# Attention outputs of a unit go raw through a DRAM scratch, are packed by DMA and normalised in packed form

## The chip, the cores and the metric

One core of a Trainium2 chip runs the whole program in one launch. The metric is the device time of one execution in microseconds. The kernel before took 4148.24 us (median of three runs, 4138.67 to 4152.86).

## What is computed

The input is a batch of 8 sequences of 1024 tokens, width 256. Four attention levels with 16 heads of width 16 read every token, every second, every fourth and every eighth; the results are merged from the coarse level to the fine one (linear upsampling, a projection, an addition), the input is added, and a layernorm follows. Then comes a feed-forward net with a gated layer, two hidden layers of 1024 and a second layernorm.

```python
for lvl in range(4):
    x = query[:, ::2 ** lvl, :]
    q, k, v = split(x @ w_in[lvl].T + b_in[lvl])          # 16 heads of 16
    attn = softmax(q @ k.T / sqrt(16))
    outs.append((attn @ v).reshape(B, S, E) @ w_out[lvl].T + b_out[lvl])
current = outs[3]
for lvl in (2, 1, 0):
    current = upsample(current) @ up_w[lvl].T + up_b[lvl] + outs[lvl]
x = layernorm(query + current)
x = layernorm(x + ffn(x))
```

## The kernel before

The attention part loops over the 8 sequences (below: batches), the feed-forward part follows. Within a batch the scores are cut into 15 **units**: 4 heads by 512 queries each (units 0 and 1 are level 2, units 2 to 5 level 1, unit 6 level 3, units 7 to 14 level 0; the coarse levels put more heads beside each other). A unit takes as many **steps** as it has tiles of 128 keys, in all 85 steps a batch: unit 0 ends at step 2, unit 3 at 12, unit 7 at 29, unit 8 at 37, unit 10 at 53, unit 12 at 69, unit 14 at 85.

What a step does: TensorE makes four matmuls for the row maxima of a unit 12 steps ahead (`p_m`, two PSUM banks, line 1196), VectorE reads each with a reduce (line 994); TensorE makes the four score matmuls (`p_s`, line 1181), ScalarE takes their exponential (`a_probs`, line 906), and TensorE multiplies by v (`p_o`, line 1213), where v has a column of ones, so that row 16 of each group of 32 partitions holds the sum of the row (spread sum). Beside these stand the projections of the next batch (line 1082), the neg rows (the maxima, transposed, placed as extra rows of q by DMA, line 647), and the merging of the levels.

After the last step of a unit: ScalarE copies `p_o` to `raw` (line 911, task `raw`). VectorE transposes raw in blocks of 32 x 32 to `attn` in two halves (`turn`, line 1023), takes the reciprocal of the sums, which now lie in column 16 of each block (`invert`, line 1027), and transposes the reciprocals, broadcast 32 times, back into `attn` (`spread`, line 1032). GpSimd multiplies `attn` by `raw` (task `attn`, line 793). SyncE then moves the 16 rows of each head with a DMA of its own to their place in `a_lo` (line 662), where the heads of a level are packed 8 to a chunk of 128 partitions. When the units of a cut are there, ScalarE makes the high part `a_hi` of it and GpSimd the low part (task `acut`, lines 915 and 798).

The order of the work is a table: `timeline` gives each task of each engine a position in steps, every engine sorts its tasks by it (with a shift by kind in `LATER`), and issues them in that order. Every wait is on a semaphore, and what stands behind a waiting instruction on the same engine waits too. All loads and stores of the attention part are issued by SyncE (SPq in the rows) on one queue: the stacks (six DMAs which gather the pieces of q and k of one or two units, line 642, task `stack`; up to 1.5 MB), the stores of the projections (line 623), chunks of the feed-forward weights that are cut in passing (`fload` line 708, `fstore` lines 712 and 713), the fetches of the last merge (lines 693 to 697), and others.

```python
LATER = {
    "act": {"proj": .3, "neg": .2, "mid": .3, "lift": .3, "acut": .5},
...
    for u, unit in enumerate(UNITS):
        p.append((unit.end + 1.3, "raw", u))
```

## Time and profile before

| | |
|---|---|
| median of the runs | 4148.24 us |
| span of the profiled execution | 4145.1 us |
| TensorE busy | 3848.4 us (93%) |
| VectorE busy | 2553.1 us (62%) |
| ScalarE busy | 2481.5 us (60%) |
| GpSimd busy | 1232.0 us (30%) |
| DMA: share of 16 engines, SyncE's and ScalarE's queue q1 | 31.4% |

The profiled execution lies within the range of the runs; its span, from the first to the last instruction, is 3.1 us below their median, and the page gives no other time for it. Shares of the whole span mix two parts: the attention part, which ends at about 2770 us, and the feed-forward part, in which TensorE is at 97% and the others at a third to 40%. A batch of the attention part starts about every 334 us; the fifth one, from which most rows come, at 1438. In the rows PE is TensorE (PEld its weight loads), DVE VectorE, ACT ScalarE, POOL GpSimd.

### The profile page before, as it was taken

Reading aid. Unit: us, or ns where it says so; the run is one execution under the profiler, and the core shown is the slowest. Engines: PE = TensorE matmul, PEld = TensorE weight load, DVE = VectorE, ACT = ScalarE, POOL = GpSimd, SP = SyncE. Lnnn points to the kernel's source line nnn. Section 1 sums busy time; section 2 is a strip of 40 time slices with the busy share of each in tenths; the row PEclk is TensorE's granted clock in tenths of the full one; section 3 lists DMA queues with packets and bytes.
Section 4 is the critical chain, followed back from the end, with each engine's and each line's share of the span. In section 5 each row is a group of like instructions: output and inputs, shape, how many; then the busy total and the mean of one; then the engine's idle time right before and its main releaser. Section 6 shows DMA issues by size and latency. Waiting matters only on the chain. (4 is left out here: it accounts for less than half of the span.)

```text
span 4145.1 us, 70266 instructions
## 1 busy us (share of the span) xinstructions
PE 3848.4 (93%) x20881; PEld 2136.6 (52%) x20881; DVE 2553.1 (62%) x4700; ACT 2481.5 (60%) x3257; POOL 1232.0 (30%) x1147
## 2 busy tenths in 40 slices
PE   6899899989989989989989998959999999999998
PEld 3334334334334333433433433327887787877887
DVE  5777877877777787787787788822333333333333
ACT  2677677767767767767766776744444443444443
POOL 2344435444444445534444443220000000000000
PEclk7999999999999999999999999979999999999999
DMA  6534535534544444453553545230000000000000
GB/s 162 165 99 108 131 90 109 122 99 94 122 115 101 108 111 110 103 127 86 116 129 89 111 114 137 64 112 1 22 11 11 12 16 16 11 12 12 21 11 11
DMA packets 283292, 331.58 MB, mean 80 GB/s; under 512 B 68562, under 2 KB 229522, under 8 KB 281120
## 3 DMA queue, kind: packets, MB, share of 16 engines
q1 hardware_dynamic: 273648, 317.73, 31.4%
q10 hardware_dynamic: 9216, 8.39, 0.6%
q8 instruction: 237, 3.88, 0.4%
q14 instruction: 191, 1.56, 0.1%
HBM read 213.81 MB, written 108.00 MB: 78 GB/s over the span
## 5 line engine op out<-in xcount | busy, mean ns | idle before, releaser
L906 ACT ACTIVATE a_probs<-a_p_s 128x1024 f32<-128x1024 f32 x1360 | 1327.1, 1021 | 606.6 <-PE a_p_s L1181 599.6
L994 DVE TENSOR_REDUCE a_part_max<-a_p_m 128x1 f32<-128x512 f32 x2048 | 1335.1, 680 | 391.1 <-PE a_p_m L1196 387.0
L1196 PE MATMUL a_p_m<-a_k_st,a_q_st 96*128 96x512 bf16 (+2 forms) x2944 | 1006.5, 376 | 155.1 <-DVE a_part_max L994 77.6
L1181 PE MATMUL a_p_s<-a_q_st,a_k_st 98*128 98x512 bf16 (+2 forms) x2944 | 824.4, 368 | 26.1 <-ACT a_probs L906 25.5
L1525 PE MATMUL p_h<-f_h_hi,f_w_hi 128*128 128x512 f32 x2048 | 808.4, 395 | 23.6 <-issue 23.6
L1525 PE MATMUL p_h<-f_h_lo,f_w_hi 128*128 128x512 f32 x2048 | 804.6, 393 | 2.1 <-issue 2.1
L1196 PEld LDWEIGHTS a_p_m<-a_k_st,a_q_st 96*128 96x128 bf16 x2944 | 257.6, 97 | 1057.3 <-DVE a_part_max L994 696.3
L1213 PE MATMUL a_p_o<-a_probs,a_v_aug 128*17 128x512 f32 (+2 forms) x5888 | 728.9, 574 | 0.0
L1496 DVE TENSOR_TENSOR f_h_lo<-f_h_f,f_h_hi 128x512 fp32r<-128x512 f32 x256 | 177.2, 692 | 701.1 <-ACT f_h_hi L1422 701.1
L994 DVE TENSOR_REDUCE a_row_max<-a_p_m 128x1 f32<-128x512 f32 (+2 forms) x672 | 439.5, 679 | 140.7 <-PE a_p_m L1196 135.4
L1420 ACT ACTIVATE f_h_f<-p_h,f_sc 128x512 f32<-128x512 f32 x256 | 176.6, 690 | 560.7 <-PE p_h L1525 560.7
L1525 PEld LDWEIGHTS p_h<-f_h_hi,f_w_hi 128*128 128x128 f32 x2048 | 389.3, 190 | 107.5 <-issue 25.6
L1525 PEld LDWEIGHTS p_h<-f_h_lo,f_w_hi 128*128 128x128 f32 x2048 | 389.3, 190 | 82.8 <-issue 2.5
L1366 POOL TENSOR_TENSOR f_rstd<-f_var_eps,f_minus_half 128x1 f32<-128x1 f32 x64 | 35.2, 550 | 1330.5 <-DVE f_var_eps L1487 1330.5
L1181 PEld LDWEIGHTS a_p_s<-a_q_st,a_k_st 98*128 98x128 bf16 x2944 | 282.2, 99 | 273.0 <-ACT a_probs L906 46.8
L779 POOL TENSOR_TENSOR a_qk_room<-a_qk_room 128x512 f32<-128x512 f32 x114 | 131.8, 1156 | 357.5 <-ACT a_qk_room L894 357.5
L1213 PEld LDWEIGHTS a_p_o<-a_probs,a_v_aug 128*17 128x17 f32 x5888 | 103.3, 96 | 225.8 <-ACT a_probs L906 127.8
L789 POOL TENSOR_TENSOR a_neg_bf<-a_neg_f,a_neg_bf 4x512 bf16<-4x512 f32 x120 | 137.9, 1150 | 273.4 <-ACT a_neg_bf L901 273.4
L1525 PE MATMUL p_h<-f_xt_hi,f_w_hi 128*128 128x512 f32 x512 | 200.4, 391 | 1.4 <-DVE f_xt_lo L1448 1.4
L1525 PE MATMUL p_h<-f_xt_lo,f_w_hi 128*128 128x512 f32 x512 | 200.1, 391 | 0.0
L793 POOL TENSOR_TENSOR a_attn<-a_raw,a_attn 128x512 f32<-128x512 f32 x120 | 153.1, 1276 | 147.5 <-DVE a_attn L1032 147.5
L1464 DVE SCALAR_TENSOR_TENSOR f_h_f<-p_h,f_sc,f_gate 128x512 f32<-128x512 f32 x128 | 96.1, 751 | 158.7 <-PE p_h L1525 138.9
(120 smaller groups left out, 4616.7 us busy)
## 6 DMA issues: line engine op xcount, KB each, us to landing
qk_scratch<-a_qk_room SPq DMA_DIRECT2D x288, 128.0 KB
a_w_lo<-wqkv_inner SPq DMA_DIRECT2D x30, 768.0 KB, 4.6
a_q_st<-qk_scratch SPq DMA_DIRECT2D x32, 384.0 KB, 5.5
a_k_st<-qk_scratch SPq DMA_DIRECT2D x32, 384.0 KB, 7.1
a_a_lo<-a_attn SPq DMA_DIRECT2D x384, 32.0 KB, 2.0
a_o_lo<-wo_inner SPq DMA_DIRECT2D x24, 512.0 KB, 3.5
a_q_st<-qk_scratch SPq DMA_DIRECT2D x88, 128.0 KB, 5.7
a_k_st<-qk_scratch SPq DMA_DIRECT2D x88, 128.0 KB, 5.7
```

The lines of the kernel that those rows point to most:

```text
L779: pool.tensor_tensor(out=rest, in0=rest, in1=bf[:, 0, :], op=ALU.subtract)\
L789: pool.tensor_tensor(out=neg_bf[:, n % 2, 1, :], in0=neg_f[:, :], in1=neg_bf[:, n % 2, 0, :], op=ALU.subtract).then_inc(neg_b.sem, 1)
L793: pool.tensor_tensor(out=attn[:, n % RING, :], in0=raw[:, n % 2, :], in1=attn[:, n % RING, :], op=ALU.mult)\
L906: act.activation(probs[:, s % 2, 2 * p:2 * p + 2, :], p_s[:, 2 * p:2 * p + 2, :], ACT.Exp, scale=HD ** -0.5).then_inc(exp_done.sem, 1)
L994: dve.reduce_max(out, src, AX.X).then_inc(max_read.sem, 1)
L1181: ins = pe.matmul(p_s[:, j, i * size:(i + 1) * size], k_st[0:ROWS + 2, spot(unit, half, j) + key:spot(unit, half, j) + key + 128], q_st[0: ...
L1196: ins = pe.matmul(p_m[:, n % 2, r * size:(r + 1) * size], q_st[0:ROWS, spot(unit, unit.blk, j) + q * 128:spot(unit, unit.blk, j) + (q + 1) ...
L1213: ins = pe.matmul(p_o[32 * j:32 * j + HD + 1, at], v_aug[:, V_TILE[lvl] + kt, unit.head + j * parts + i, :], probs[:, n % 2, j, at], start ...
L1420: act.activation(h_f[:, v % 2, :], p_h[:, v % 4, :], ACT.Gelu, scale=sc[:, 8 + v:9 + v]).then_inc(deep_read.sem, 1)
L1464: dve.scalar_tensor_tensor(out=h_f[:, v % 2, :], in0=p_h[:, (2 * v + 1) % 4, :], scalar=sc[:, 8 + v:9 + v], in1=gate[:, v % 2, :], op0=ALU ...
L1496: dve.tensor_tensor(out=h_lo[:, (half + v // 8) % 2, v % 8, :], in0=h_f[:, v % 2, :], in1=h_hi[:, (half + v // 8) % 2, v % 8, :], op=ALU.s ...
L1525: ins = pe.matmul(out, a, c, start=first and n == 0, stop=last and n == len(terms) - 1)
```

## The change

The output of a unit is no longer turned and normalised in place. Each of the 15 units of a batch now goes this way (positions in steps after the end of the unit):

- `raw` (+1.3, ScalarE) copies `p_o` to one of three `raw` buffers.
- `spill` (+2.3, SyncE) writes that buffer, 256 KB, to `raw_scr` in DRAM.
- `pack` (+3.1, SyncE) waits until the spill has landed. It reads the four rows of sums back as `den`, 128 partitions x 16 values (8 KB), and then moves the rows of the heads from DRAM to `a_lo`, one DMA for a unit of level 1 or 0, four for the others.
- `invert` (+3.9, VectorE) waits for den and takes one reciprocal, 128 x 16.
- `rspill` (+4.4, SyncE) waits for it and writes the 8 KB to `rec_scr` in DRAM.
- `rload` (+5.2, SyncE) waits for that landing and loads each reciprocal row broadcast to 16 partitions into `share`.
- `norm` (+6.2, GpSimd, once for each of the 9 cuts of a batch) multiplies `a_lo` by `share`; `acut` (+6.5, before +6.4) makes the high and low parts of the product.

The tasks `turn`, `spread` and `attn` are gone. The buffers `attn` (3 x 512 columns) and one pair of `raw` give room for three `raw`, `den`, `rec` and `share`.

```diff
-PACKS = [HG * across(unit.lvl) for unit in UNITS]
+PACKS = [1 if across(unit.lvl) == 1 else HG for unit in UNITS]
+SHARE_AT = (0, W // 2, W, 0, W, 0, W, 0, W)
+SHARE_FREED = (-1, -1, 0, 2, 3, 4, 5, 6, 7)
+SHARES = [max(1, HG * across(unit.lvl) // 8) for unit in UNITS]
...
-    "sp": {"proj": 2.2, "neg": 1.6, "attn": 1.8, "finish": 1, "keep": .5},
+    "sp": {"proj": 2.2, "neg": 1.6, "finish": 1, "keep": .5},
...
         p.append((unit.end + 1.3, "raw", u))
-        p += [(unit.end + 1.55 + .3 * part, "turn", 2 * u + part) for part in range(2)]
-        p.append((unit.end + 2.05, "invert", u))
-        p += [(unit.end + 2.35 + .3 * part, "spread", 2 * u + part) for part in range(2)]
-        p.append((unit.end + 2.75, "attn", u))
+        p += [(unit.end + 2.3, "spill", u), (unit.end + 3.1, "pack", u), (unit.end + 3.9, "invert", u)]
+        p += [(unit.end + 4.4, "rspill", u), (unit.end + 5.2, "rload", u)]
...
-    p += [(max(UNITS[u].end for u in cut.units) + 6.4, "acut", n) for n, cut in enumerate(CUTS)]
+    for n, cut in enumerate(CUTS):
+        p += [(max(UNITS[u].end for u in cut.units) + 6.2, "norm", n), (max(UNITS[u].end for u in cut.units) + 6.5, "acut", n)]
...
+                        elif kind == "spill":
+                            slot = n % RING
+                            sp.wait_ge(raw_done.sem, raw_done.value(it, n + 1))
+                            packed[slot].wait(sp, it, PACKED[n - RING] if n >= RING else 0)
+                            den_in[slot].wait(sp, it, n // RING)
+                            sp.dma_start(raw_scr[slot, :, :], raw[:, slot, :]).then_inc(spilled[slot].sem, 16)
+                        elif kind == "pack":
+                            spilled[slot].wait(sp, it, n // RING + 1)
+                            rec_done.wait(sp, it, max(n - RING + 1, 0))
+                            sp.dma_start(den[:, slot, :], raw_scr[slot, HD::32, :].rearrange("j (r t) -> j r t", t=HG * W // 128)).then_inc(den_in[slot].sem, 16)
                             a_freed(sp, it, unit.lvl)
+                            if parts == 1:
+                                to = unit.head % 8 * HD
+                                sp.dma_start(a_lo[to:to + HG * HD, unit.head // 8, at:at + size].bitcast(F32), by_head).then_inc(packed[slot].sem, 16)
...
+                        elif kind == "rspill":
+                            sp.wait_ge(rec_done.sem, rec_done.value(it, n + 1))
+                            shared[slot].wait(sp, it, SHARED[n - RING] if n >= RING else 0)
+                            sp.dma_start(rec_scr[slot, :].rearrange("(p t) -> p t", p=128), rec[:, slot, :]).then_inc(rec_spilled[slot].sem, 16)
+                        elif kind == "rload":
+                            rec_spilled[slot].wait(sp, it, n // RING + 1)
+                            a_lo_done.wait(sp, it, SHARE_FREED[cut])
+                            for c in range(SHARES[n]):
+                                sp.dma_start(share[to:to + heads * HD, SHARE_AT[cut] + c * size:SHARE_AT[cut] + (c + 1) * size],
+                                             src.unsqueeze(1).broadcast_to((heads, HD, size))).then_inc(shared[slot].sem, 16)
...
-                            pool.wait_ge(spread_done.sem, spread_done.value(it, 2 * n + 2))
-                            pool.tensor_tensor(out=attn[:, n % RING, :], in0=raw[:, n % 2, :], in1=attn[:, n % RING, :], op=ALU.mult)\
+                        elif kind == "norm":
+                            for u in CUTS[n].units:
+                                packed[u % RING].wait(pool, it, PACKED[u])
+                                shared[u % RING].wait(pool, it, SHARED[u])
+                            pool.tensor_tensor(out=part, in0=a_part(a_lo, CUTS[n]).bitcast(F32), in1=part, op=ALU.mult)\
...
-                            dve.transpose(attn[:, u % RING, cols], raw[:, u % 2, cols]).then_inc(turned_done.sem, 1)
                         elif kind == "invert":
-                            dve.wait_ge(turned_done.sem, turned_done.value(it, 2 * n + 2))
-                            dve.reciprocal(rec[:, :], attn[:, n % RING, :].rearrange("p (c r) -> p c r", r=32)[:, :, HD]).then_inc(rec_done.sem, 1)
+                            den_in[n % RING].wait(dve, it, n // RING + 1)
+                            rec_spilled[n % RING].wait(dve, it, n // RING)
+                            dve.reciprocal(rec[:, n % RING, :], den[:, n % RING, :]).then_inc(rec_done.sem, 1)
```

**First place: SyncE at the start of a batch, around the full stack for units 7 and 8.** Before, SyncE's list there reads (L642 is the stack, L662 the moves of `a_attn` to `a_a_lo`, L647 the neg rows, the first four L662 of unit 14, the eight of unit 0):

```order
L642 DMA a_q_st<-qk_scratch 48x4x1024
L642 DMA a_k_st<-qk_scratch 48x4x1024
L642 DMA a_q_st<-qk_scratch 32x4x1024
L642 DMA a_k_st<-qk_scratch 32x4x1024
L642 DMA a_q_st<-qk_scratch 16x4x1024
L642 DMA a_k_st<-qk_scratch 16x4x1024
L662 DMA a_a_lo<-a_attn 16x512 x4
L647 DMA a_q_st<-a_neg_bf 1x4x512 x2
L662 DMA a_a_lo<-a_attn 16x256 x8
```

Now (L670 is the spill of unit 0, L701 the spill of the reciprocals of unit 14, L654 the same stack, L680 den of unit 0, L692 its packing, L714 the broadcast load of unit 14):

```order
L670 DMA raw_scratch<-a_raw 128x512
L701 DMA rec_scratch<-a_rec 128x16
L654 DMA a_q_st<-qk_scratch 48x4x1024
L654 DMA a_k_st<-qk_scratch 48x4x1024
L654 DMA a_q_st<-qk_scratch 32x4x1024
L654 DMA a_k_st<-qk_scratch 32x4x1024
L654 DMA a_q_st<-qk_scratch 16x4x1024
L654 DMA a_k_st<-qk_scratch 16x4x1024
L680 DMA a_den<-raw_scratch 128x1x16
L692 DMA a_a_lo<-raw_scratch 32x1x256 x4
L714 DMA a_share<-rec_scratch 64x1x512
```

The spill of unit 0 stands ahead of the stack and its den behind it, and a wait for VectorE's reciprocal of unit 14 stands ahead of the stack.

**Second place: SyncE around the next full stack, at unit 3.** Before (L708 loads a chunk of feed-forward weights):

```order
L642 DMA a_q_st<-qk_scratch 16x4x1024
L642 DMA a_k_st<-qk_scratch 16x4x1024
L708 DMA a_qk_room<-wf 128x1024
L737 DMA x<-a_c_f 128x256
```

Now (L670 and L680 are spill and den of unit 3, L760 the chunk):

```order
L654 DMA a_q_st<-qk_scratch 16x4x1024
L654 DMA a_k_st<-qk_scratch 16x4x1024
L670 DMA raw_scratch<-a_raw 128x512
L760 DMA a_qk_room<-wf 128x1024
L789 DMA x<-a_c_f 128x256
L680 DMA a_den<-raw_scratch 128x1x16
L687 DMA a_a_lo<-raw_scratch 64x1x512
```

Spill, chunk and den of unit 3 all stand behind the stack, in this order.

**Third place: VectorE after a unit.** Before, one unit's work between the maxima (L994):

```order
L1023 STREAM_TRANSPOSE a_attn<-a_raw 128x256
L994 TENSOR_REDUCE a_row_max<-a_p_m 128x1
L1023 STREAM_TRANSPOSE a_attn<-a_raw 128x256
L994 TENSOR_REDUCE a_row_max<-a_p_m 128x1
L1027 RECIPROCAL a_rec<-a_attn 128x16
L994 TENSOR_REDUCE a_row_max<-a_p_m 128x1
L994 TENSOR_REDUCE a_row_max<-a_p_m 128x1
L1032 STREAM_TRANSPOSE a_attn<-a_rec 128x256
L994 TENSOR_REDUCE a_row_max<-a_p_m 128x1
L1032 STREAM_TRANSPOSE a_attn<-a_rec 128x256
```

Now (L1049 are the maxima):

```order
L1049 TENSOR_REDUCE a_row_max<-a_p_m 128x1
L1049 TENSOR_REDUCE a_row_max<-a_p_m 128x1
L1049 TENSOR_REDUCE a_row_max<-a_p_m 128x1
L1077 RECIPROCAL a_rec<-a_den 128x16
L1049 TENSOR_REDUCE a_row_max<-a_p_m 128x1
L1049 TENSOR_REDUCE a_row_max<-a_p_m 128x1
```

Of five instructions one is left; it stands 3.9 steps after the end of the unit instead of 2.05, and reads `den`.

## Rows read from the trace of the kernel before

**Rows 1.** A stretch of 350 us: us, busy us (x instructions) by engine, clock, DMA, GB/s

```profile
1100.00:1450.00 350.00, 325.48 (x1996) 135.69 (x1994) 273.24 (x506) 250.39 (x315) 154.61 (x139) 0.98 0.48 111
```

**Rows 2.** Groups of instructions of the attention part: busy us, mean ns | idle before, releasers

```profile
L994 DVE TENSOR_REDUCE a_part_max<-a_p_m 128x1 f32<-128x512 f32 x2048 | 1335.1, 680 | 391.1 <-PE a_p_m L1196 387.0
L1196 PE MATMUL a_p_m<-a_k_st,a_q_st 96*128 96x512 bf16 (+2 forms) x2944 | 1006.5, 376 | 155.1 <-DVE a_part_max L994 77.6 <-DVE a_row_max L994 42.8 <-issue 17.7
...
L994 DVE TENSOR_REDUCE a_row_max<-a_p_m 128x1 f32<-128x512 f32 (+2 forms) x672 | 439.5, 679 | 140.7 <-PE a_p_m L1196 135.4
...
L1023 DVE STREAM_TRANSPOSE a_attn<-a_raw 128x256 f32<-128x256 f32 x240 | 103.2, 431 | 55.6 <-ACT a_raw L911 54.6
L1032 DVE STREAM_TRANSPOSE a_attn<-a_rec 128x256 f32<-128x256 f32 x240 | 103.0, 430 | 0.1
```

**Rows 3.** Timeline of PE, value matmuls: start, length, engine; two plain steps, two with transposes

```profile
1550.76 1.05 PE L1213 MATMUL a_p_o<-a_probs,a_v_aug 128*17 128x512 f32 x8
1553.89 1.05 PE L1213 MATMUL a_p_o<-a_probs,a_v_aug 128*17 128x512 f32 x8
...
1590.64 1.05 PE L1213 MATMUL a_p_o<-a_probs,a_v_aug 128*17 128x512 f32 x8
1594.04 1.05 PE L1213 MATMUL a_p_o<-a_probs,a_v_aug 128*17 128x512 f32 x8
```

**Rows 4.** Timeline at unit 8: its raw, and VectorE's maxima up to 3.9 steps

```profile
1588.40 0.60 ACT L911 ACTIVATE a_raw<-a_p_o 128x512 f32<-128x512 f32 x1 [0.75 <-PE a_p_o L1213]
...
1595.45 1.34 DVE L994 TENSOR_REDUCE a_part_max<-a_p_m 128x1 f32<-128x512 f32 x2 [0.27 <-PE a_p_m L1196]
```

**Rows 5.** DMA issues of the whole run: count, KB each, median us to landing

```profile
a_a_lo<-a_attn SPq DMA_DIRECT2D x384, 32.0 KB, 2.0
...
up_near<-a_d_room SPq DMA_DIRECT2D x8, 512.0 KB, 5.9
...
a_o_lo<-wo_inner SPq DMA_DIRECT2D x8, 256.0 KB, 2.6
...
f_sc<-scales SPq DMA_DIRECT2D x1, 17.0 KB, 1.8
```

**Rows 6.** Landing of a_a_lo's moves issued in 1477:1480, in 1446:1450, in 1656:1660

```profile
DMA to landing us min/median/max: 1.9/2.0/2.0
...
DMA to landing us min/median/max: 8.2/8.4/8.8
...
DMA to landing us min/median/max: 3.4/3.7/3.9
```

**Rows 7.** SyncE around the stack at 1486 to 1492, and the chunk's landing

```profile
1486.53 0.34 SPq L642 DMA_DIRECT2D a_q_st<-qk_scratch  x1
...
1488.83 0.43 SPq L642 DMA_DIRECT2D a_k_st<-qk_scratch  x1
1489.94 0.37 SPq L708 DMA_DIRECT2D a_qk_room<-wf  x1
...
a_qk_room<-wf SPq DMA_DIRECT2D x1, 512.0 KB, 10.0
```

**Rows 8.** Timeline at unit 0: first DMA of the stack, VectorE up to 3.9 steps

```profile
1444.52 0.32 SPq L642 DMA_DIRECT2D a_q_st<-qk_scratch  x1
...
1451.66 0.65 DVE L994 TENSOR_REDUCE a_row_max<-a_p_m 128x1 f32<-128x512 f32 x1
```

**Rows 9.** Timeline at unit 3: VectorE up to 3.9 steps, TensorE's score matmul after

```profile
1491.22 1.27 DVE L994 TENSOR_REDUCE a_part_max<-a_p_m 128x1 f32<-128x512 f32 x2
...
1501.97 1.03 PE L1181 MATMUL a_p_s<-a_q_st,a_k_st 98*128 98x512 bf16 x2 [2.72 <-ACT a_probs L906]
```

**Rows 10.** Timeline of VectorE: at unit 10 up to 3.9 steps, and after unit 7

```profile
1655.14 1.34 DVE L994 TENSOR_REDUCE a_part_max<-a_p_m 128x1 f32<-128x512 f32 x2 [0.27 <-PE a_p_m L1196]
...
1567.75 1.29 DVE L994 TENSOR_REDUCE a_part_max<-a_p_m 128x1 f32<-128x512 f32 x2 [2.77 <-PE a_p_m L1196]
```

**Rows 11.** Two stretches after a wait; columns as in rows 1, the clock third from the end

```profile
1502.00:1505.00 3.00, 3.00 (x12) 1.02 (x16) 1.37 (x3) 3.00 (x5) 2.82 (x3) 0.50 0.04 6
1833.00:1843.00 10.00, 8.01 (x27) 3.08 (x28) 5.96 (x13) 7.08 (x11) 6.72 (x6) 0.50 0.34 113
```

## What the change will do to the time, forecast before it ran

> **What bounds the kernel now.** I read the stretches of the program first, then the groups of instructions, then the timeline of one batch, then the landing times of the DMAs. The attention part (0 to about 2770 us, eight batches of some 334 us) is where the change lies; the feed-forward part behind it is untouched. In a full stretch of it TensorE is busy 93% of the time, VectorE 78%, ScalarE 72% [rows 1]. No engine is at 100%: TensorE and VectorE pass work through two PSUM banks (`p_m`), and each waits for the other. VectorE waited 387.0 + 135.4 us for a row-maximum matmul, TensorE 77.6 + 42.8 us for VectorE's read of one [rows 2]. A step that holds nothing else takes 3.13 us; a step in which VectorE also does transposes takes 3.40 us [rows 3]. So VectorE work between the maxima is on the path, but only with 0.3 us a step. More important: every engine runs its list in order, so an instruction on VectorE that waits for a DMA stops the maxima, and with them TensorE after two banks.
>
> **What the change takes away.** Per unit VectorE loses two transposes of raw (0.43 us each) and two spreading transposes (0.43 each), 103.2 + 103.0 us in all [rows 2]. The reciprocal stays, in the same shape (128x16), but on other data. GpSimd's multiply of 120 units becomes one of 72 cuts; GpSimd is busy 154.6 of 350 us [rows 1], so I count that at nothing. What the transposes cost on the path: 136 of the 680 steps (17 a batch, by the timeline) have them and no projection beside, which is where TensorE isn't the longer one; 136 x 0.3 = 41 us. Steps with a projection take 4.2 us with or without transposes. From both sides: nothing at least, and at most all of TensorE's waits for VectorE, 77.6 + 42.8 = 120 us [rows 2]. I take 41 because it is counted in steps.
>
> **What it adds: a chain of DMAs with VectorE in the middle.** Before, raw went from ScalarE to VectorE directly. Now it is raw (ScalarE), spill of 256 KB to DRAM, den of 8 KB back, reciprocal (VectorE), spill of 8 KB, broadcast load of 128 KB, product (GpSimd). The first two of the four landings come before a VectorE instruction, the reciprocal, which stands 3.9 steps behind the unit's end in the list. How long has that chain? In a quiet unit (unit 8 of the fifth batch) raw is done at 1589.0 and VectorE reaches that place at 1596.8, 7.8 us later [rows 4]. What the chain needs when the queue is empty: 0.3 to issue, 2.6 for 256 KB, 0.2, 2.0 for a small one [rows 5], together 5.1. That leaves 2.7 us; quiet units lose nothing. The bounds of the two landings together are 2.0 + 2.0 and 5.9 (a 512 KB store) + 2.0 [rows 5]; I take 2.6 + 2.0, since 256 KB has a row of its own, if one of a load.
>
> The DMA queue is not always empty. All these DMAs are issued by SyncE on one queue, and a small one behind a large one lands late: the four 32 KB moves at 1477 landed after 1.9 to 2.0 us, the same moves at 1447 to 1449, just behind a stack (the gather of q and k pieces, up to 1.5 MB), after 8.2 to 8.8, those behind two smaller stacks after 3.4 to 3.9 [rows 6]. A chunk of weights issued at 1489.94 behind the stack that was issued from 1486.53 on (six DMAs, the last 2.7 us later) took 10.0 us [rows 7]. So I looked for units whose spill or den stands behind a stack in SyncE's new list:
>
> - Unit 0: its den is behind the 1.5 MB stack, which follows the spill (first order piece in the part on the change). The stack was issued from 1444.5 and is now some 1.5 us later, as the reciprocal spill of unit 14 stands ahead of it. Den issued at 1448.9, plus 8.4 [rows 6] = 1457.3. VectorE is at that place at 1452.3 [rows 8]: 5.0 us.
> - Unit 3: spill behind the stack of 1486.5 to 1489.3, the chunk load behind the spill, den behind that load (second order piece). The chunk landed at 1499.9 before; with 256 KB more ahead and den behind it, about 1502.2. VectorE gets there at 1492.5 [rows 9]: 9.7 us late. But in this place the old kernel has a hole already (ScalarE waited for that chunk, the next score matmul began at 1501.97 after 2.72 us [rows 9]), in which it was two steps further on. Two steps are 6 to 7 us, so I count 6 of the 9.7.
> - Unit 10: spill behind one half-size stack, den behind the other. Spill issued about 1651, landed about 1656.3, den on the queue that then has 3.7 us of landing [rows 6] and a 256 KB spill more: 1661.5. VectorE is there at 1656.5 [rows 10]: 5.0.
> - Unit 12: its spill follows two stacks and two 512 KB stores (5.9 us each [rows 5]). The queue clears 7 us after raw; plus 1.3 for the spill and 2.2 for den is 10.5 against 8.1: 2.4.
> - Unit 7: behind a full stack, clears 10 us after raw, den 12.0 against 8.7: 3.3, of which 1.6 falls into a wait that is there anyway (VectorE idle 2.77 us until 1567.75 [rows 10]): 1.7.
>
> After that wait TensorE ran at 0.50 of its clock, that is 1.2 instead of 2.4 GHz, from 1502 to 1505, and a batch later in the same place from 1833 to 1843 [rows 11]; half of such a stretch, 1.5 to 5 us, is lost. Units 3 and 7 have that already; units 0 and 10 get it new, 2.5 us each.
>
> Per batch 5.0 + 6.0 + 5.0 + 2.4 + 1.7 + 5.0 = 25.1 us. Units 10 and 12 of the last batch have no next batch's stacks behind them (-9.9): 8 x 25.1 - 9.9 = 191 us. At the end of attention nothing covers the longer chain of unit 14 (two landings of 2 us more, less 1.7 us of transposes), but the last steps win a little elsewhere; I count nothing.
>
> SyncE's issues: 80 moves of attn a batch become 24 packing moves, 45 (spill, den, reciprocal spill: 15 each) and 16 loads, 85. Same number, no cost; its waits now stand ahead of the placing of neg rows, of stacks and of stores. Most of those have steps to spare; I count nothing, and up to 3 us a batch if the cover is gone. The broadcast load and the product come before ScalarE's cut at 7.0 steps behind the unit's end; with 3.1 steps (10 us) after the reciprocal for 2.0 + 2.6 + 1.1 us they are hidden.
>
> **Sum.** 191 - 41 = +150 us. The profiled execution has a span of 4145.1, 3.1 us under the median of 4148.2; whatever lies around the span is unchanged. 4148 + 150 = 4298 us.
>
> The Trainium skill (DMA: Bandwidth & Descriptors, Specifications) says that transfers in pieces below 512 B make the DMA engine read, modify and write, which would speak against den: its destination takes 64 B a partition. Here the nearest row is the load of the scales, 136 B a partition, that landed in 1.8 us [rows 5], no later than a small move in 512 B or longer pieces; by the trace it costs nothing, and by the rule den alone would be later in all 15 units.
>
> **Rivals.**
> 1. *The landings hide, relief is all that is left (faster).* If den lands before VectorE reaches the reciprocal also behind stacks, place by place (it decides at 2.7 us of extra landing), only the 41 us of relief count: 4148 - 41 = 4107, and 4028 if all 120 us went. For it: ten of the fifteen units of a batch have a quiet queue and 2.7 us to spare. Against: 8.2 to 8.8 instead of 2.0 in the very place of unit 0 [rows 6].
> 2. *Every unit is late.* If a 256 KB store takes 5.9 us rather than 2.6 [rows 5], the quiet chain needs 8.4 of 7.8 to 9.7 us, some 0.5 us in eight of the ten quiet units, and the five others get 3.3 more each: +21 a batch, 4298 + 8 x 21 = 4466. For it: the only large stores to DRAM in the trace are slow ones. Against: they were two at once. The Trainium skill (DMA: Bandwidth & Descriptors, Anatomy of one DMA) says that completion waits for the receipt of the write and that this is longest where the target is HBM; by it this rival, not the forecast, has the spill right, and the store of 5.9 us agrees, though two loaded the queue.
> 3. *Holes overlap.* The new waits take in waits that are there already, as in units 3 and 7, and the clock doesn't fall anew: unit 0 and 10 at 3 us, unit 3 at 2, nothing else, 8 x 8 = 64 less 41 = +23, 4171; between 4140 and 4230. For it: VectorE idles in every batch anyway. Against: it idles in other places than the three named.
>
> **Chances.** Forecast 0.55 (its own range 4235 to 4370), rival 1 0.13, rival 2 0.14, rival 3 0.18. The range 4160 to 4410 leaves out rival 1, a part of rival 3 below 4160 and most of rival 2's upper half, about 0.2 in all. A measurement of this kernel tells 0.3% (12 us) from no change. Faster: rival 1 and a hundredth of rival 3, 0.14; within 0.3%: a third of rival 3, 0.06; slower 0.80.
>
> **What would show it.** Right: in the profile after, VectorE's reciprocal is waited for, idle before it is 15 to 25 us a batch with a DMA (den from the raw scratch) as releaser, longest in units 3, 0 and 10, 5 to 10 us each; TensorE's clock falls twice more a batch; steps with a reciprocal but no stack near take 3.15 to 3.25 instead of 3.40 us; the batch takes 350 to 355 us instead of 334. Wrong: den landing in 3 us behind the stack; no idle before the reciprocal; or waits of SyncE that put off the neg rows, so that score matmuls are late in places that I haven't named.

## The result, and the profile after

The changed kernel takes 4405.3 us (median of 4 runs, 4399.3 to 4411.4) against 4150.6 us for the kernel before (4 runs beside it): a ratio of 1.062, 95% interval 1.060 to 1.064. The profiled execution of it is the one of 4411.4 us, span 4409.6, which is 264.5 us more than the span before. The forecast was +150 us, 4298 us in a range of 4160 to 4410: the direction was right, and so was the mechanism of the largest waits, but the size was 105 us too small. The measured time lies 5 us inside the upper end of that range and outside the 4235 to 4370 that the forecast gave itself with a chance of 0.55, between it and rival 2; the profiled execution, the slowest of the four, is above 4410. That the range held it is luck of its width.

The page of the changed kernel, part 5 (busy us, mean ns | idle before, releaser) and part 6 (KB, median us to landing):

```profile
L962 ACT ACTIVATE a_probs<-a_p_s 128x1024 f32<-128x1024 f32 x1360 | 1328.8, 1020 | 832.7 <-PE a_p_s L1225 826.2
L1049 DVE TENSOR_REDUCE a_part_max<-a_p_m 128x1 f32<-128x512 f32 x2048 | 1330.5, 687 | 469.0 <-PE a_p_m L1240 463.2
L1240 PE MATMUL a_p_m<-a_k_st,a_q_st 96*128 96x512 bf16 (+2 forms) x2944 | 1029.9, 386 | 363.0 <-DVE a_part_max L1049 197.5
...
L1077 DVE RECIPROCAL a_rec<-a_den 128x16 f32<-128x16 f32 x120 | 30.3, 252 | 369.1 <-DMA a_den<-raw_scratch 365.0
...
raw_scratch<-a_raw SPq DMA_DIRECT2D x120, 256.0 KB, 4.8
```

The reciprocal works for 30.3 us in all and is waited for for 365.0 us, by a DMA. What it holds up stands in the rows above it: before the row-maximum matmuls, which VectorE's reads release, TensorE was idle for 155.1 us [rows 2] and is idle for 363.0 now, and ScalarE's exponentials wait for score matmuls for 826.2 us. The same stretch as in [rows 1], columns as there:

```profile
1100.00:1450.00 350.00, 303.98 (x1800) 124.64 (x1792) 232.63 (x404) 229.42 (x285) 138.00 (x127) 0.94 0.47 117
...
1585.70:1593.90 8.20, 0.00 (x0) 0.00 (x0) 0.82 (x3) 0.00 (x0) 0.82 (x1) 0.50 0.64 133
1593.90:1599.40 5.50, 5.46 (x19) 3.77 (x20) 2.55 (x4) 2.68 (x3) 1.90 (x2) 0.50 0.56 214
```

TensorE does 1800 matmuls in 350 us where it did 1996. The two lower rows are one pause and what follows it: the granted clock is 0.50, the lower level of 1.2 GHz, for 8.2 us in which TensorE does nothing and for 5.5 us more in which it is busy. Over the six middle batches there are 6.7 such stretches a batch where there were 2.0; they last 47.2 us a batch (13.7 before), and TensorE is busy for 31.1 us of them (12.2 before). The mean granted clock of the span fell from 0.971 to 0.938.

Unit 0 of the fifth batch in the timeline (start, length, engine [idle before <-releaser]):

```profile
1577.35 0.58 SPq L670 DMA_DIRECT2D raw_scratch<-a_raw  x1
1578.14 0.32 SPq L701 DMA_DIRECT2D rec_scratch<-a_rec  x1
1579.27 0.32 SPq L654 DMA_DIRECT2D a_q_st<-qk_scratch  x1
...
1582.96 0.55 SPq L680 DMA_DIRECT2D a_den<-raw_scratch  x1
...
1593.08 0.25 DVE L1077 RECIPROCAL a_rec<-a_den 128x16 f32<-128x16 f32 x1 [10.26 <-DMA a_den<-raw_scratch]
1593.25 1.23 DVE L1049 TENSOR_REDUCE a_row_max<-a_p_m 128x1 f32<-128x512 f32 x2
...
1593.94 0.61 PE L1240 MATMUL a_p_m<-a_k_st,a_q_st 96*128 96x512 bf16 x1 [9.69 <-DVE a_row_max L1049]
```

As forecast: the 8 KB den stands behind the six DMAs of the stack and is back 10.1 us after its issue, VectorE stands still, and TensorE with it. Two things were not forecast. The spill itself goes out 3.4 us after raw's end (1574.0): SyncE stood until 1574.5 for unit 14's spill to land, and then issued that unit's den and packing and a chunk of weights before it. And unit 4 of the same batch waits as well (its spill goes out 5.4 us after raw's end, behind four loads, a spread load and two 512 KB stores):

```profile
1656.31 0.37 SPq L765 DMA_DIRECT2D w_hi_scratch<-a_qk_room  x1
1657.03 0.66 SPq L670 DMA_DIRECT2D raw_scratch<-a_raw  x1
...
1665.50 0.57 SPq L680 DMA_DIRECT2D a_den<-raw_scratch  x1
...
1667.76 0.25 DVE L1077 RECIPROCAL a_rec<-a_den 128x16 f32<-128x16 f32 x1 [6.50 <-DMA a_den<-raw_scratch]
```

Within a batch I number the 85 steps from 0, by TensorE's value matmuls, and call the number the place; a place lasts from the start of its first value matmul to that of the next place. Where the 264.5 us are: 2.3 before the first step, 30.6 in the first batch, 196.4 in the six middle ones (333.8 us each before, 366.5 now), 20.6 in the last up to its place 82, 14.5 from there to the end of the program. Mean of the six middle batches, us:

| place | what stands there | before | after | difference | forecast, clock included |
|---|---|---|---|---|---|
| 2, 4 | unit 14's and unit 0's reciprocal | 7.7 | 20.2 | +12.5 | 7.5 |
| 14 to 16 | unit 3's; chunk of weights | 18.6 | 23.3 | +4.6 | 6.0 |
| 18 | unit 4's | 3.7 | 9.8 | +6.0 | 0 |
| 31 | unit 7's | 3.3 | 7.3 | +4.1 | 1.7 |
| 55 | unit 10's | 3.3 | 10.1 | +6.9 | 7.5 |
| 71 | unit 12's | 3.3 | 6.9 | +3.7 | 2.4 |
| all others | shorter steps | | | -5.1 | -5.1 |
| batch | | 333.8 | 366.5 | +32.7 | +20.0 |

### The profile page after: what moved, and what is told of

It is laid out like the page before. It is cut to its first block and busy times, and to the rows that moved or that the text cites. A ratio compares the mean times of both kernels' runs of the same rounds, so it can differ in the third digit from the quotient of the medians.

```text
span 4409.6 us, 71122 instructions
## 1 busy us (share of the span) xinstructions
PE 3914.6 (89%) x20881; PEld 2163.3 (49%) x20881; DVE 2414.9 (55%) x4220; ACT 2484.3 (56%) x3257; POOL 1158.8 (26%) x1099
## 5 line engine op out<-in xcount | busy, mean ns | idle before, releaser
L962 ACT ACTIVATE a_probs<-a_p_s 128x1024 f32<-128x1024 f32 x1360 | 1328.8, 1020 | 832.7 <-PE a_p_s L1225 826.2
L1049 DVE TENSOR_REDUCE a_part_max<-a_p_m 128x1 f32<-128x512 f32 x2048 | 1330.5, 687 | 469.0 <-PE a_p_m L1240 463.2
L1240 PE MATMUL a_p_m<-a_k_st,a_q_st 96*128 96x512 bf16 (+2 forms) x2944 | 1029.9, 386 | 363.0 <-DVE a_part_max L1049 197.5
L1225 PE MATMUL a_p_s<-a_q_st,a_k_st 98*128 98x512 bf16 (+2 forms) x2944 | 853.0, 380 | 0.9 <-ACT a_probs L962 0.7
L1049 DVE TENSOR_REDUCE a_row_max<-a_p_m 128x1 f32<-128x512 f32 (+2 forms) x672 | 437.2, 687 | 161.9 <-PE a_p_m L1240 157.8
L1225 PEld LDWEIGHTS a_p_s<-a_q_st,a_k_st 98*128 98x128 bf16 x2944 | 292.2, 102 | 252.7 <-issue 34.3
L1077 DVE RECIPROCAL a_rec<-a_den 128x16 f32<-128x16 f32 x120 | 30.3, 252 | 369.1 <-DMA a_den<-raw_scratch 365.0
```

Of the source, the lines that this page charges most:

```text
L962: act.activation(probs[:, s % 2, 2 * p:2 * p + 2, :], p_s[:, 2 * p:2 * p + 2, :], ACT.Exp, scale=HD ** -0.5).then_inc(exp_done.sem, 1)
L1049: dve.reduce_max(out, src, AX.X).then_inc(max_read.sem, 1)
L1225: ins = pe.matmul(p_s[:, j, i * size:(i + 1) * size], k_st[0:ROWS + 2, spot(unit, half, j) + key:spot(unit, half, j) + key + 128], q_st[0: ...
L1240: ins = pe.matmul(p_m[:, n % 2, r * size:(r + 1) * size], q_st[0:ROWS, spot(unit, unit.blk, j) + q * 128:spot(unit, unit.blk, j) + (q + 1) ...
```

## Experiments

All ratios are to the kernel before, run beside them (its median was 4145 to 4151 us).

**relief**, of the kernel before:

```diff
-  dve.transpose(attn[:, u % RING, cols], raw[:, u % 2, cols]).then_inc(turned_done.sem, 1)
+  dve.sem_inc(turned_done.sem, 1)
-  dve.transpose(attn[:, u % RING, cols], rec[...].broadcast_to((128, W // 64, 32))).then_inc(spread_done.sem, 1)
+  dve.sem_inc(spread_done.sem, 1)
```

> The kernel before with the turn and spread transposes left out on VectorE (each replaced by its semaphore increment alone; the reciprocal reads the raw copy and GpSimd multiplies raw by raw, so the normalisation is not computed). Everything else of the kernel before stays, its eight small packing DMAs too. Theory (the relief term of the forecast): steps that carried transposes fall from 3.41-3.47 us to 3.13, 136 steps x 0.3 = 41 us, so about 4110 us; the chain of the change is in it nowhere. Rival: the transposes were on no limiting chain, 4140 to 4155 us. Rival the other way: the step falls by more, up to 120 us, 4030 us.

Measured: 4113.4 us, ratio 0.991 (0.989 to 0.992), 37 us less. The plain steps with a reciprocal fell to a median of 3.13 us. The relief term (41) stands.

**nowait**, of the changed kernel:

```diff
-  den_in[n % RING].wait(dve, it, n // RING + 1)
+  dve.wait_ge(raw_done.sem, raw_done.value(it, n + 1))
...
-  dve.reciprocal(rec[:, n % RING, :], den[:, n % RING, :])
+  dve.tensor_copy(rec[:, n % RING, :], raw[:, n % RING, 0:HG * W // 128])
   SyncE ahead of its store of rec, and ScalarE ahead of its copy to raw:
+  den_in[slot].wait(sp, it, n // RING + 1)
+  rec_done.wait(act, it, max(n - RING + 1, 0))
```

> The changed kernel, but VectorE does not wait for the spread sums that come back from DRAM: in place of the short reciprocal it copies 16 columns of the raw output as soon as the raw output is there (so the normalisation is not computed). Every DMA of the change stays, and SyncE and GpSimd wait for the same landings as before. Theory (VectorE's wait in its queue ahead of the score maxima is the whole loss, as forecast, only larger): the 345 to 369 us idle ahead of the reciprocal go, the half-clock stretches with them, and the kernel runs at 4105 to 4150 us. Rival A (the added traffic, 0.75 MB and more a unit, or SyncE's own waits delay stacks and fetches for other engines): 4200 to 4350 us. Rival B (the holes are filled again by the next wait in line, GpSimd's on the spread reciprocals): 4300 us or more.

Measured: 4303.0 us, ratio 1.037 (1.035 to 1.039). Theory missed; both rivals are within their numbers. VectorE's wait is gone and only 102 of 255 us come back. (The last line of the edit, which keeps raw from being overwritten, is a wait of the experiment's own, 15.5 us of ScalarE's time over 400 to 2750 us, and may hold back a part.) The middle batches take 352.0 us. The longest steps are now at places 6 (10.1 us), 15 and 16 (10.0 and 11.1). Place 6 in the timeline of nowait:

```profile
1538.62 1.26 POOL L852 TENSOR_TENSOR a_share<-a_a_lo,a_share 128x512 f32<-128x512 f32 x1 [9.38 <-DMA a_share<-rec_scratch]
1539.92 0.63 ACT L973 ACTIVATE a_a_hi<-a_share 128x512 fp32r<-128x512 f32 x1 [10.38 <-POOL a_share L852]
...
1541.52 1.03 PE L1228 MATMUL a_p_s<-a_q_st,a_k_st 98*128 98x512 bf16 x2 [5.94 <-ACT a_probs L964]
```

Read it upwards: TensorE waits for ScalarE's exponentials, which stand behind ScalarE's cut, which waits for GpSimd's product, which waits for the spread load. The other end of the chain of DMAs holds the kernel in its turn.

**late**, of the changed kernel, for units 0 to 12 (`norm` and `acut` by 3 as well):

```diff
-  (unit.end + 3.9, "invert", u), (unit.end + 4.4, "rspill", u), (unit.end + 5.2, "rload", u)
+  (unit.end + 6.9, "invert", u), (unit.end + 7.4, "rspill", u), (unit.end + 8.2, "rload", u)
```

> The changed kernel with one thing moved: reciprocal, its store, its spread load, and the normalising multiply and the cut behind them stand 3 steps later in every queue for units 0 to 12 (units 13 and 14 as they were). Nothing is left out. Theory (only the place in VectorE's queue is wrong: the sums are back up to 11 us after it, and 3 steps are 9.4 us): nearly all of the wait before the reciprocal goes, 4110 to 4150 us, at or below the kernel before, since the transposes stay gone. Rival A (a later norm delays the output projection that needs the cuts, GpSimd or ScalarE waits in its place): 4180 to 4300 us. Rival B (traffic is the cause): above 4300 us.

Measured: 4375.1 us, ratio 1.053 (1.052 to 1.055). Theory missed; it is rival A in kind, with a larger loss (the number alone would suit rival B, traffic, which spread rules out below). VectorE's wait for den falls from 300.8 to 37.9 us (both over 400 to 2850 us), and 30 us come back. ScalarE's wait for the product, in the same stretch:

```profile
ACT a_a_hi L976 <- POOL a_share L856: 155.6, 30, 10.8
...
DVE a_rec L1083 <- DMA a_den<-raw_scratch: 37.9, 13, 4.4
```

It was 39.6 us in the changed kernel. As reciprocal and product moved by the same 3 steps, the room between them stayed as it was.

**stack**, of the changed kernel, in the table of stacks:

```diff
-  7: 4.5, 8: 14
+  7: 5.6, 8: 15.6
```

> The changed kernel with two 1.5 MB stacks of SyncE moved a little later: stack 7 from step 4.5 to 5.6 and stack 8 from step 14 to 15.6, so that the store and the small load of the sums of units 0 and 3 stand ahead of them in SyncE's queue. Theory (the chain of units 0 and 3 is late because its DMAs queue behind the stack: 9.6 and 10.8 us of wait a batch): the waits of units 0 and 3 fall to 0 to 3 us, other units unchanged; 14 to 20 us a batch with the clock's share, 8 batches, so 4250 to 4300 us. Rival (the engines are busy in any case, or the stack comes too late for the scores that need it, so that TensorE waits instead): 4350 to 4420 us.

Measured: 4428.1 us, ratio 1.066 (1.065 to 1.068), 23 us slower than the changed kernel and 8 us above even the rival's range. And yet the cause that the theory names is confirmed at its place: unit 0's wait falls from 9.6 to 1.4 us a batch, unit 3's from 10.8 to 0.3. But now unit 1's spill is behind the stack, and its wait goes from 0.0 to 10.6 us:

```profile
1583.81 0.55 SPq L680 DMA_DIRECT2D a_den<-raw_scratch  x1
1586.07 0.25 DVE L1077 RECIPROCAL a_rec<-a_den 128x16 f32<-128x16 f32 x1 [1.85 <-DMA a_den<-raw_scratch]
...
1591.36 0.34 SPq L670 DMA_DIRECT2D raw_scratch<-a_raw  x1
...
1602.20 0.60 SPq L680 DMA_DIRECT2D a_den<-raw_scratch  x1
1605.02 0.25 DVE L1077 RECIPROCAL a_rec<-a_den 128x16 f32<-128x16 f32 x1 [11.19 <-DMA a_den<-raw_scratch]
```

The pause in TensorE moved from place 4 (15.5 us) to place 6 (15.5). At the other stack place 14 fell from 14.6 to 3.8 us, but place 16 took 17.0 us instead of 4.4, and there another chain had come behind the stack, the store of x (the merged rows, `a_c_f`):

```profile
1652.45 1.26 POOL L892 TENSOR_TENSOR a_c_f<-a_d_room 128x512 f32<-128x512 f32 x1 [12.72 <-DMA x<-a_c_f]
...
1657.48 0.69 DVE L1092 TENSOR_REDUCE lo_max<-a_qk_room 128x1 f32<-128x512 f32 x1 [11.23 <-POOL a_qk_room L898]
1658.82 0.61 PE L1240 MATMUL a_p_m<-a_k_st,a_q_st 96*128 96x512 bf16 x1 [11.02 <-DVE a_part_max L1049]
```

GpSimd waits for the store of x, VectorE's look at a chunk of weights (`lo_max`) waits for GpSimd, and the maxima stand behind it. So the wait was not only handed to the neighbour unit.

**traffic**, of nowait; SyncE's waits for `spilled`, `den_in` and `rec_spilled` go to GpSimd ahead of `norm`:

```diff
-  spilled[slot].wait(sp, it, n // RING + 1)
...
-  sp.dma_start(den[:, slot, :], raw_scr[slot, HD::32, :]...)
+  sp.dma_start(den[:, slot, :], raw_scr[RING + slot, HD::32, :]...)
```

> As nowait, and in addition SyncE waits for none of the chain's own landings: the loads of the sums, of the raw heads and of the spread reciprocals read other places in DRAM that were filled once at the start (so neither the attention output nor the normalisation is the right one), and what SyncE waited for is waited for by GpSimd ahead of the normalising multiply. All DMAs stay, in number, size and shape. Nothing but traffic, SyncE's issue time and GpSimd's and ScalarE's later waits is left of the change. Theory (the 153 us that nowait still loses against the kernel before are waits in SyncE's queue, which issue the packing loads, the stacks and the weight chunks late, and which then hold GpSimd and ScalarE): 4110 to 4160 us, some 5 us of it the filling at the start. Rival (the traffic itself, 0.5 MB and more a unit, makes stacks and chunks land late): 4250 to 4300 us, no better than nowait.

Measured: 4236.6 us, ratio 1.021 (1.018 to 1.024), 66 us less than nowait: between the two expectations. SyncE's waits for its own landings are a real part, but not all; places 6 (10.4 us), 15 and 16 (10.3 and 9.7) are still long, with ScalarE's cut waiting for the product for 135.7 us.

**nowait_norm**, of nowait:

```diff
-  (max(UNITS[u].end for u in cut.units) + 6.2, "norm", n), (... + 6.5, "acut", n)
+  (NORM_AT[n], "norm", n), (NORM_AT[n] + .3, "acut", n)
+  NORM_AT = (14.2, 16.2, 23.2, 26.4, 27.4, 56.2, 64.2, 85.7, 93.3)
```

> As nowait, and the normalising multiply on GpSimd and the cut on ScalarE and GpSimd behind it stand later in the queues: by 6 steps for cuts 0 and 1, 5 for cuts 2, 5 and 6, 2.5 for cut 7, 2 for cut 8 (not in the last batch), cuts 3 and 4 as they were. Theory (ScalarE waits in front of its cut for GpSimd's multiply, that for the spread reciprocals, up to 10.9 us, and the exponentials are queued behind): the 10 us step at place 6 of a batch falls to about 4 us, the one at place 2 to 4 and the one at 55 by a few, some 10 us a batch, so 4200 to 4240 us. The long steps at places 15 and 16, which wait for a weight chunk that SyncE issued late, stay at 10 to 11 us. Rival (what ends those long steps is the late landing of stacks, not the cut): 4280 to 4310 us, as nowait.

Measured: 4282.5 us, ratio 1.032 (1.030 to 1.034): at the edge of the rival's range, 20 us below nowait. ScalarE's wait for the product went from 124.7 to 13.9 us and place 6 from 10.1 to 3.3, but of those 6.8 us a batch only 1.4 are left at the batch's end (350.6): places 8, 10, 11, 19, 20 and 55 each took 0.4 to 1.3 us more.

**norm_only**, of the changed kernel: the same lines as nowait_norm, the reciprocal where it was.

> The changed kernel, nothing left out, with only the multiply and the cut later (as in nowait_norm), the reciprocal where the change put it. Theory (the waits are in line behind one another: while VectorE still waits 44 us a batch for the sums, the room given to the cut is worth little): 4370 to 4410 us. Rival (ScalarE's wait for the multiply is an equal part of the loss, additive to VectorE's): 4300 to 4350 us.

Measured: 4411.5 us, ratio 1.064 (1.061 to 1.066): no gain at all, as the theory says in kind, 1.5 us above its range. ScalarE's wait for the product is 3.5 us, VectorE's for den 302.2.

**spread**, of the changed kernel, all links drawn apart:

```diff
   steps behind the unit's end of pack, invert, rspill, rload:
-  (3.1, 3.9, 4.4, 5.2)
+  (4.2, 6.2, 6.9, 7.9) if u not in (5, 6, 13, 14) else (3.6, 4.7, 5.1, 5.8) if u < 7 else (4, 5.4, 6, 7)
+  NORM_AT = (14.2, 16.2, 23.2, 26.4, 27.4, 56.2, 64.2, 85.7, 93.3)
```

> The changed kernel with its whole chain drawn out, nothing left out. For units 0 to 4 and 7 to 12: loads of the sums 1.1 steps later, reciprocal 2.3, its store 2.5, the spread load 2.7 later; units 5 and 6 by 0.5 to 0.8; 13 and 14 by 0.9 to 1.8 (not in the last batch); multiply and cut as in nowait_norm. So every link stands behind its predecessor's landing in the queue of its engine. Theory (all of the loss is links that wait in queues ahead of other work): the three long waits (VectorE for the sums, ScalarE for the multiply, SyncE for its own landings) go to less than a third, 4130 to 4200 us. If only VectorE's and ScalarE's places matter and SyncE's queue stays late: 4200 to 4260. Rival (traffic): above 4280 us.

Measured: 4160.5 us, ratio 1.0023 (1.0013 to 1.0033): 245 of the 255 us are back, with every DMA and every multiply of the change in place. Middle batches take 335.7 us (in a profiled execution that is the slowest of 11, 4181.4 us). Its waits over 400 to 2750 us:

```profile
ACT a_a_hi L982 <- POOL a_share L862: 39.4, 14, 5.4
...
DVE a_rec L1089 <- DMA a_den<-raw_scratch: 37.5, 16, 25.1
```

(25.1 of the 37.5 are one wait in the last batch, where TensorE had work: that batch took 289.0 us against 286.8.) The time is the theory's, its signs only in part: it had all three waits fall to less than a third, and VectorE's did (290.6 us in the changed kernel over the same stretch), but ScalarE's for the product did not (33.9), nor did SyncE's for its spills, reciprocals and their stores (598.4 to 417.6, over 400 to 2850 us). How long a wait is says little; what stands behind it decides.

The traffic, rival of four expectations, is not the cause of the 255 us. But spread has the relief of 37 us in it and is still 9 us slower than the kernel before, so what is left of the chain, its traffic included, costs some 46 us, 15 of them at the program's end.

**spread2**, of spread; **spread3**, of spread2; **chunk_before**, spread3's lines in the kernel before:

```diff
   spread2, steps behind the unit's end, and the cuts' places:
-  14: (4, 5.4, 6, 7), 6: (3.6, 4.7, 5.1, 5.8), NORM_AT[8]: 93.3, NORM_AT[4]: 27.4
+  14: (3.6, 4.8, 5.3, 5.9), 6: (3.6, 4.7, 5.1, 6.1), NORM_AT[8]: 93.8, NORM_AT[4]: 28.6
   spread3 and chunk_before:
+  more = 1.3 if n == PER_BATCH - 1 else 0
-  mine = [(at + by, kind, k, n) for kind, by in steps_of_chunk]
+  mine = [(at + by + (more if by else 0), kind, k, n) for kind, by in steps_of_chunk]
```

> As spread, with two corrections, nothing left out: unit 14's chain a little earlier (0.4 to 1.1 steps, so its spread load is out before stack 7 and unit 0's reciprocal) and its multiply 0.5 step later; unit 6's spread load behind the loads of x and of the weights, its multiply 1.2 steps later. Theory (the steps of 7.3 and 6.4 us at places 7 and 8 are ScalarE's cut waiting for that multiply, the 9 us step at place 30 in half the batches weights that SyncE issued late): 5 to 7 us a batch less at places 7 and 8, 1 to 2 at 30, less some 2 us where the output projection now waits: 4115 to 4140 us, below the kernel before. Rival (those steps wait for something else): 4150 to 4170.

> As spread2, and of the third weight chunk of a batch all but its load stands 1.3 steps later (cut, rest, maxima, stores). Theory (the two long steps at places 15 and 16, 5.5 and 8.7 us in spread, are ScalarE waiting for the chunk and VectorE's maxima waiting for GpSimd's rest): 4 to 7 us a batch less than spread2, 4070 to 4110 us. Rival (the hole only moves with the chunk): as spread2.

> The kernel before with the same shift of the third weight chunk alone, nothing left out, so that what spread3 gains by it is not put down to the change. Theory: the steps of 7.4 and 7.5 us at places 15 and 16 shrink to 4 to 5 each, 4100 to 4125 us. Rival: the hole moves with the chunk, 4140 to 4160 us.

Measured: spread2 4212.0 us (1.016, 1.015 to 1.018), worse than spread by 51: theory missed. Unit 6's later product met the projection that needs it (place 28: 3.1 us in spread, 9.0 here), and unit 14's reciprocals were stored right behind stack 7:

```profile
1482.09 0.43 SPq L713 DMA_DIRECT2D rec_scratch<-a_rec  x1
...
1491.82 0.54 SPq L726 DMA_DIRECT2D a_share<-rec_scratch  x1
```

SyncE stood from 1482.5 to 1491.8 for the landing of 8 KB. spread3 took 4186.7 us (1.010, 1.009 to 1.012), 25 less than spread2, places 15 and 16 together 10.0 instead of 15.6: the chunk part of its theory holds, the level doesn't. chunk_before took 4111.2 us (0.992, 0.991 to 0.993), theory right: 14.9 us at places 15 and 16 became 8.0.

**spread4**, of spread, with the chunk's shift and units 5 and 6 as in the change:

```diff
-  14: (4, 5.4, 6, 7), 0: (4.2, 6.2, 6.9, 7.9), 1: (4.2, 6.2, 6.9, 7.9), stack 7: 4.5
+  14: (3.1, 4.2, 4.6, 5.5), 0: (3.2, 6.2, 6.9, 7.9), 1: (4.6, 6.6, 7.1, 8.1), stack 7: 5.7
```

> As spread, nothing left out, with units 5 and 6 and cuts 3 and 4 back where the change put them, the third weight chunk 1.3 steps later (as in chunk_before), and around the batch's start unit 14's loads, reciprocal, store and spread load and unit 0's loads all ahead of stack 7, which goes from step 4.5 to 5.7. Theory (in spread2 the store of unit 14's reciprocals stood behind stack 7's 1.5 MB and SyncE then waited 9.7 us for it): places 6 to 8 of a batch take 12 to 14 us in all (spread 17.6), places 15 and 16 10 (14.3), place 30 5.1 (7.0), so 325 to 330 us a batch: 4075 to 4115 us, below the kernel before (and near the 4111 us of chunk_before, which has the chunk's part of this gain without the change). Rival (what lands behind stack 7 is now unit 1's store, and SyncE waits there, as in stack): 4130 to 4170 us.

Measured: 4165.5 us, ratio 1.0044 (1.0031 to 1.0058): in the rival's range, and by its mechanism only in part. Places 15 and 16 (8.5 us) and 30 (4.7) fell as expected. SyncE did stand for unit 1's store, from 1469.1 to 1476.5 in the fifth batch, as the rival says. But what TensorE waited for at place 6 (10.7 us), in every batch, was stack 7 itself, which was now late:

```profile
1476.07 1.03 PE L1253 MATMUL a_p_m<-a_k_st,a_q_st 96*128 96x512 bf16 x2 [6.90 <-DMA a_k_st<-qk_scratch]
```

No version of the change beat the kernel before; chunk_before, without it, did by 0.8%.

## Why the forecast was right in sign and short in size

- **Relief, 41 us.** Right: 37 measured alone (relief). The step in which it was counted falls from 3.40 to 3.13 us [rows 3], 0.27 and not 0.3, and 136 x 0.27 is 37.
- **Quiet units lose nothing.** Right where the queue is quiet. In units 2, 8 and 9 den is issued 2.2 to 2.4 us after the spill, close to the 2.6 I took from the 256 KB load [rows 5], and the reciprocal finds it there. But of the ten units that I had counted as quiet only these and unit 5 find a quiet queue; in the other six the spill takes 4.3 to 8.0 us to land (unit 14's, for one, stands behind a stack that I hadn't looked at), and three of them wait: unit 4 5.9 us a batch, unit 13 2.0, unit 14 1.8. The page's median of 4.8 is that of spills with something ahead of them. Rival 2 (every store slow, 5.9) is out by these units. The Trainium skill (DMA: Bandwidth & Descriptors, Anatomy of one DMA), which I had behind that rival, holds the receipt of an HBM write for the longest; in the quiet units no such extra is to be seen beside the load. That section is about DMAs that GpSimd issues; these are SyncE's.
- **Units behind a stack.** The mechanism is shown by the experiment stack, where the wait follows the stack. The terms: unit 10 with its clock 6.9 for 7.5, unit 3 net 4.6 for 6.0 (its wait did swallow an older pause, as I had counted), unit 12 3.7 for 2.4. The term that was mis-sized most is unit 0 with the clock, 12.5 for 7.5 (unit 14's wait of 1.8 us included). I had added SyncE's new issues ahead of den but not its new waits: den left at 1583.0, 9.0 us after raw, where my count gave some 5.
- **The failed step: "its waits now stand ahead of [...]; I count nothing".** I had set 0 to 3 us a batch for SyncE. With VectorE's wait taken away, doing away with SyncE's own waits for the chain's landings gives 66 us, some 8 a batch (nowait against traffic). For unit 0 the rows agree: its spill leaves 3.3 us after raw's end in the changed kernel, 2.2 in nowait and 0.4 in traffic. What costs is where they stand, not how long they are: over 400 to 2850 us SyncE waits 339.6 us for spills to land, 128.2 for stores of the reciprocal and 130.6 for the reciprocal itself, but before it waited 363.8 us for GpSimd's product, and all its waits together went only from 985.5 to 1050.4 us.
- **Unit 4, for which I had nothing.** It is the largest part of what a batch lost above the forecast, 6.0 us. Its spill leaves 5.6 us after raw's end and takes 8.0 to land. In the fifth batch the rows lead back to SyncE's wait for unit 3's spill (until 1642.5), behind which a store of x stood that held GpSimd for 12.30 us. But in traffic, where SyncE waits for no such landing, unit 4's spill leaves even later, 9.7 us after raw's end, and takes 7.6. So that SyncE's waits are the cause here is not shown; what both kernels have is the list itself: ahead of this spill stand the fetches of the merge, for which SyncE waits for GpSimd (11.8 us in the fifth batch of traffic), and two 512 KB stores. Unit 7 (4.1 for 1.7) is another case: its spill leaves 0.4 us after raw's end and lands 10.2 us later, behind the stack.
- **"They are hidden": spread load, product, cut.** Wrong in kind, though it cost little in the changed kernel as it stood, because VectorE's wait came first: 39.6 us of ScalarE's wait there, 124.7 once VectorE's was gone. norm_only and nowait against nowait_norm show the two are in line, not additive: the same room for the product returned nothing in the one and 20 us in the other.
- **"At the end of attention I count nothing."** Wrong by 14.5 us, and in every kernel with the change it is 11.5 to 18.5. Place 82 of the last batch takes 6.9 us more, because ScalarE waits for unit 13's product with the last exponentials behind it. From the last raw's start to the last projection matmul it took 17.8 us before and takes 31.4, 13.6 more. Some 6 us come back between that matmul and the end. The rows of the changed kernel:

```profile
2987.01 0.63 ACT L970 ACTIVATE a_a_hi<-a_share 128x512 fp32r<-128x512 f32 x1 [9.99 <-POOL a_share L850]
2987.55 1.92 ACT L962 ACTIVATE a_probs<-a_p_s 128x1024 f32<-128x1024 f32 x2
...
2995.34 0.57 ACT L967 ACTIVATE a_raw<-a_p_o 128x512 f32<-128x512 f32 x1
2996.14 0.33 SPq L670 DMA_DIRECT2D raw_scratch<-a_raw  x1
...
3004.94 3.54 SPq L749 DMA_DIRECT2D a_fine_room<-up_far  x4
3008.67 0.56 SPq L714 DMA_DIRECT2D a_share<-rec_scratch  x1
3017.15 1.26 POOL L850 TENSOR_TENSOR a_share<-a_a_lo,a_share 128x512 f32<-128x512 f32 x1 [14.36 <-DMA a_share<-rec_scratch]
...
3020.56 0.55 PE L1126 MATMUL a_p_a<-a_o_hi,a_a_hi 128*128 128x256 f32 x1 [25.09 <-POOL a_a_lo L854]
```

  The spread load leaves 7 us after the reciprocal's store, behind eight other issues, and GpSimd gets it 8 us later still, behind their data. I had counted bare landings.
- **Clock.** I gave 2.5 us to each of two new falls. For one fall that was about right: after unit 0's pause TensorE is busy for 5.46 us at 0.50, and half of that is 2.7. But there are 4.7 new falls a batch and not two. TensorE is busy at the lower level for 31.1 us a batch instead of 12.2; half of the difference, 9.5 us, is an estimate of what the clock takes, against 5.0 in the forecast. It is inside the places' differences above; how it divides among them, no run separates.
- **The other rivals.** Rival 1 is out: den behind a stack was 7 to 8 us later than on a quiet queue. Of rival 3 what it says of unit 3 is right, as the forecast had it too; units 0 and 10 had no old wait to fall into.
- **The signs that I had named.** The reciprocal is waited for, with den as releaser, but for 44.5 us a batch and not 15 to 25; longest in units 3 and 0 as named, then in unit 4 before unit 7 and unit 10. The batch takes 366.5 us, not 350 to 355. Steps with a reciprocal and nothing else take 3.13 to 3.14 us. Of the signs of being wrong one came true in part: a place that I hadn't named, unit 4's.

The sum by measured terms: the six middle batches lost 196.4 us, the first and the last 30.6 and 20.6, so 247.6; with 14.5 at the end and 2.3 at the start, 264.4. Of the 12.7 us a batch by which the middle ones lie above the forecast, unit 4 is 6.0, unit 0 5.0, unit 7 2.4 and unit 12 1.3; units 3 and 10 came out 1.4 and 0.6 lower. What stays open: which single link of spread returns how much. Taken away one by one, VectorE's wait returned 102 us, then SyncE's 66 or the product's 20; of the 142 us between nowait and spread the other 56 came only with all links moved together. Open too is what makes up the 46 us that spread's chain still costs.

## What to carry to other kernels

Where a value goes through DRAM and back between engines that run lists in order, every link is a place where a queue can stand still, the issuing engine's own queue too. Give each link its own room behind the landing before it; moving the first waiting instruction alone only hands the wait to the next (late, nowait), and moving a large transfer out of the way hands it to a neighbour (stack, spread4). Before pricing such a chain as hidden, list what is issued between its links, at the program's end too, where nothing is left to hide it.

## What the runs showed of the hardware

- A DMA of 8 KB issued behind 1.5 MB on one queue is waited for for some 9 to 10 us, a load in the changed kernel (1582.96 to 1593.08) as well as a store in spread2 (1482.5 to 1491.8); on a quiet queue a load of it took at most 2.7 us (2998.32 to 3000.98).
- A store of 256 KB to DRAM landed in 2.0 to 2.1 us in the quiet units (2, 5, 8 and 9 of the changed kernel), in 10.2 behind a full stack (unit 7), and in 4.8 in the median.
- The change adds 49 MB of DMA in all (317.7 to 366.9 MB on q1), 0.41 MB a unit. Once its links had room (spread) all of the chain together cost at most some 46 us.
- Den's pieces of 64 B a partition cost little: where VectorE waited for a den with nothing large ahead of it, 2.2 to 2.4 us from issue to reciprocal, against 2.0 to landing for the 32 KB moves before [rows 5], as the forecast had read from the load of the scales.
